# First attention of a four-layer kernel: row units dealt out anew over the twelve steps of a batch

## What is computed

```python
q = hidden @ Wq + bq                       # 56 x 256 a batch, 32 heads of 8
k = encoder @ Wk + bk                      # 1500 x 64, 8 heads of 8
v = encoder @ Wv + bv
scores = einsum('bkgld,bksd->bkgls', q, k) * scale + mask
attn = softmax(scores, axis=-1)            # over the 1500 context rows
out = einsum('bkgls,bksd->bkgld', attn, v)
x = layernorm(out @ Wo + bo + hidden)
```

## Time and profile before

| | |
|---|---|
| median of 3 runs | 3276.99 us (3270.93 to 3280.79) |
| profiled execution | 3270.37 us |
| its span | 3268.5 us |
| mean granted TensorE clock | 0.941 |
| TensorE busy | 2863.0 us (88%) |
| VectorE busy | 2012.5 us (62%) |
| ScalarE busy | 1415.9 us (43%) |
| GpSimd busy | 661.8 us (20%) |

### The profile page before, as it was taken

The page is one execution under the profiler, slowest core; times in us unless marked ns, Lnnn a source line. Parts: engine busy times, 40 slices in busy tenths (PEclk is TensorE's granted clock), DMA queues, the critical chain, the costliest instruction groups (busy, mean ns, idle before and its releaser), DMA issues. The chain is left out here.

```text
span 3268.5 us, 63507 instructions
## 1 busy us (share of the span) xinstructions
PE 2863.0 (88%) x18753; PEld 1515.8 (46%) x18753; DVE 2012.5 (62%) x4195; ACT 1415.9 (43%) x3023; POOL 661.8 (20%) x483
## 2 busy tenths in 40 slices
PE   5799999999999999999867888699999997888885
PEld 3344444444444444444334444356666664544443
DVE  3667677676767767677447887344454440168775
ACT  2255555555555555565622221254544443212221
POOL 5221221121122122112023333000000001033331
PEclk8699999999999999999978999799999998999997
DMA  6333333432433343243010000111111100100000
GB/s 198 106 83 114 108 112 85 121 108 76 120 108 105 91 121 108 75 121 102 16 63 1 1 1 1 47 34 28 33 32 29 32 17 30 60 1 6 6 1 12
DMA packets 117235, 205.18 MB, mean 63 GB/s; under 512 B 39765, under 2 KB 84546, under 8 KB 116546
## 3 DMA queue, kind: packets, MB, share of 16 engines
q1 hardware_dynamic: 116930, 201.08, 21.5%
HBM read 156.09 MB, written 44.59 MB: 61 GB/s over the span
## 5 line engine op out<-in xcount | busy, mean ns | idle before, releaser
L586 DVE CUSTOM_DVE_ANT_0 masked<-ps_a,mask 112x750 f32<-112x750 f32 x1024 | 941.7, 936 | 377.8 <-PE ps_a L473 369.1
L546 ACT ACTIVATE probs<-ps_a 128x448 f32<-128x448 f32 (+1 forms) x1536 | 743.3, 542 | 546.6 <-PE ps_a L439 542.8
L473 PE MATMUL ps_a<-ks,q_row 96*112 96x375 bf16 x2048 | 530.1, 342 | 58.0 <-DVE part_max L586 35.6
L439 PE MATMUL ps_a<-q_sc,ks 99*128 99x448 bf16 (+1 forms) x1536 | 450.5, 359 | 50.0 <-ACT probs L546 28.5
L459 PE MATMUL ps_a<-probs,vp 128*32 128x224 f32 x6144 | 378.4, 364 | 1.2 <-ACT probs L546 0.9
L473 PEld LDWEIGHTS ps_a<-ks,q_row 96*112 96x112 bf16 x2048 | 220.6, 133 | 329.8 <-issue 271.0
L2024 DVE CUSTOM_DVE_ANT_0 f_masked<-ps_c,f_mp 112x432 f32<-112x432 f32 x256 | 145.6, 605 | 221.3 <-PE ps_c L1876 218.7
L439 PEld LDWEIGHTS ps_a<-q_sc,ks 99*128 99x128 bf16 (+1 forms) x1536 | 132.5, 100 | 281.3 <-issue 232.5
L236 POOL CAST k_piece<-kv_t 64x1500 bf16<-64x1500 f32 x32 | 45.6, 1426 | 1042.8 <-ACT kv_t L228 1042.6
L459 PEld LDWEIGHTS ps_a<-probs,vp 128*32 128x32 f32 x6144 | 164.3, 111 | 160.0 <-ACT probs L546 60.8
L215 PE MATMUL ps_a<-ctx_t,wkv 128*128 128x375 f32 x512 | 198.6, 514 | 21.0 <-DVE x_nat L347 10.8
(11 more groups left out here) (283 smaller groups left out, 3978.3 us busy)
## 6 DMA issues: line engine op xcount, KB each, us to landing
ctx_t<-in_ctx_t SPq DMA_DIRECT2D x32, 1500.0 KB, 8.8
ks<-k_scr SPq DMA_DIRECT2D x64, 562.5 KB, 5.1
mask<-in_mask SPq DMA_DIRECT2D x64, 328.1 KB, 5.4
k_scr<-k_piece SPq DMA_DIRECT2D x64, 281.2 KB, 6.5
k_scr<-k_piece SPq DMA_DIRECT2D x64, 187.5 KB, 6.8
f_context<-in_ctx_t SPq DMA_DIRECT2D x32, 375.0 KB, 3.1
k_scr<-k_piece SPq DMA_DIRECT2D x64, 93.8 KB, 7.1
q_row<-q_scr SPq DMA_DIRECT2D x64, 84.0 KB, 4.5
```

The source lines that it names most:

```text
L439: mm = pe.matmul(out, ks[par][:, j, at], q_sc[par][:, j], start=True, stop=not with_mask)
L473: mm = pe.matmul(ps[0:2 * L, bank + i, 0:SC], q_row[which][:, j, h, gp * 2 * L:(gp + 1) * 2 * L], ks[which][0:SROWS, j, at], start=True, s ...
L546: act.activation(probs[t % 2][0:n, i], ps[0:n, k % SCORE_BANKS, 0:PW] .rearrange("p (h n) -> p h n", h=2), ACT.Exp).then_inc(probs_done, 1)
L586: dve.tensor_tensor_reduce(out=masked[:, u % 2], in0=two_banks(bank, 2 * L), in1=in_two(mask[which][:, c * SU:(c + 1) * SU]), scale=1.0, s ...
```

## The change

The table of row units and the order within a step change. Steps 0, 6, 7 and 11 have two row units instead of three, steps 3, 4, 5 and 10 four instead of three; the others keep their number. In the steps with four, one stands at place 0, one at place 1 (ahead of the second score pair), and then at place 2 a row, the `kv` or `out` unit, and the fourth row. In the steps with two, one stands at place 0 and one at place 2, behind the second score pair. Step 9 keeps its three at places 0, 1 and 2. The number of units in the list is 40 before and after, and so is the rule of the two bank pairs.

| step | 0 | 1 | 2 | 3 | 4 | 5 | 6 | 7 | 8 | 9 | 10 | 11 |
|---|---|---|---|---|---|---|---|---|---|---|---|---|
| rows before | 3 | 2 | 2 | 3 | 3 | 3 | 3 | 3 | 1 | 3 | 3 | 3 |
| rows after | 2 | 2 | 2 | 4 | 4 | 4 | 2 | 2 | 1 | 3 | 4 | 2 |
| other unit | | den | turn | kv | out | kv | | | kv | neg | kv | |

```diff
--- before.py
+++ after.py
@@ -51,7 +51,7 @@
 
 
 EARLY_ROWS = 9
-ROWS_AT = {9: 3, 10: 3, 11: 3, 0: 3, 1: 2, 2: 2, 3: 3, 4: 3, 5: 3, 6: 3, 7: 3, 8: 1}
+ROWS_AT = {9: 3, 10: 4, 11: 2, 0: 2, 1: 2, 2: 2, 3: 4, 4: 4, 5: 4, 6: 2, 7: 2, 8: 1}
 OTHERS_AT = {1: ("den", -1, 0), 2: ("turn", 1, 0), 3: ("kv", 3, 0), 4: ("out", -1, 0), 5: ("kv", 3, 1),
              8: ("kv", 3, 2), 10: ("kv", 3, 3)}
 NEG_STEP = 9
@@ -67,10 +67,13 @@
         if t == NEG_STEP:
             units.append((t, 0, "neg", 1, 0))
         units.append((t, 0) + mine[0])
+        rest = mine[1:]
+        if len(rest) == 3 or (len(rest) == 2 and t not in OTHERS_AT):
+            units.append((t, 1) + rest.pop(0))
+        units += [(t, 2) + m for m in rest[:1]]
         if t in OTHERS_AT:
-            units += [(t, 2) + m for m in mine[1:2]] + [(t, 2) + OTHERS_AT[t]] + [(t, 2) + m for m in mine[2:]]
-        else:
-            units += [(t, 1) + m for m in mine[1:2]] + [(t, 2) + m for m in mine[2:]]
+            units.append((t, 2) + OTHERS_AT[t])
+        units += [(t, 2) + m for m in rest[1:]]
     return units
```

## The result

The changed kernel takes 3314.49 us (median of 4 runs, 3312.42 to 3316.19) against 3274.34 (3270.93 to 3280.79): a ratio of 1.0127, 95% interval 1.0107 to 1.0146. It is slower by 40 us, where 22 was forecast (3299, from the median of 3276.99 then known). The time lies inside the stated range (3281 to 3319), but nearer to rival B's 3320 than to the forecast. The profiled span is 3314.3 us, 45.8 longer than before.

What follows compares the result with a forecast made beforehand. TensorE's fixed issue order was taken as bound, held by row banks (1.79 us) and the exponential loop (2.33). Costs 2.98 less savings 2.16 gave 0.82 a batch, +22 with smaller terms: 3299, range 3281 to 3319.

Steps and rivals of the forecast that it cites:

- rival B: ScalarE paces two-row steps; steps 6 to 8 save just 0.74, steps 0 and 1 nothing: +43 us, 3320; 14%.
- the named signs: Key products 1.8 us behind added rows; steps 6, 7: 2.4–2.6; 3, 5, 10: 5.1–5.4; 4: 5.8; batch: 47.6 us.
- Added rows beside key products: Steps 3, 5, 10: product waits for its bank behind the fourth row; 0.67 us each, 2.01 a batch.
- Step 4: Output product starts 1.79 us behind the added row, nothing returns behind it: cost 0.97 us a batch.
- Steps 6 to 8: Two-row steps 6 and 7 lose the row bank's hold; 9.80 us together falls by 1.42.
- What is late next is the exponential loop, 2.33 us, so it just fits: Step 7: scores, exponentials, value product, next scores take 2.33 us, within the forecast step of 2.41.
- Steps 0 and 1: Second scores of step 0 and the accumulator copy come earlier: 0.37 us saved a batch, bounds 0 and 0.55.
- step 11: Last step of a batch, one row unit fewer: saving 0.37 us of 4.18, bounds 0 and 0.45.
- The loop's jump: Step 0 behind the jump, once in four batches at half clock: removed row saves 0.3 more, 1.8 us in all.
- Rival A: Key and output products don't wait on the added row; each four-row step pays just 0.37: -20 us, 3257; 10%.
- Rival C: Additional cold-clock stretches per batch or per four batches, 2.3 us each: +14 to +55, some 3330 with the forecast; 6%.
- Rival D: Little difference: full returns behind key products, larger savings in steps 0 and 1 and 6 to 8: 3280 to 3291; 14%.

Runs made afterwards that it cites:

- Alone: Kernel before with one row unit moved from step 7 to step 4, other steps unchanged: 3283.29 us, ratio 1.0031.
- The half exponential: Changed kernel with ScalarE's exponentials on 224 of 448 columns, the value product taking that half twice: 3291.24 us, ratio 1.0055.
- the last experiment: Kernel before with product first in three-row steps 3, 5, 10, and one mask branch per batch instead of one per score pair: 3476.05 us, ratio 1.0631.
- the first experiment: Changed kernel with the key or output product first behind the second scores in steps 3, 4, 5, 10, both remaining rows after it: 3325.24 us.
- the same order with the branch ahead of each pair: Kernel before, own row counts; in steps 3, 5, 10 second row before second scores, key product right behind them, then third row: 3249.84 us.

## Why the prediction was right in kind and short in size

The four stands came where they were forecast, and the kernel got slower by them. The size was short: batch 22 grew by 1.80 us where the steps summed to 0.82, and that 3314 us is inside the range is owed to an upper bound that had been widened for rival B. Of the named signs, steps 3 and 5 came in their bounds and step 7 at the edge (2.61); steps 6 (2.68), 10 (5.52) and 4 (5.93) and the batch (48.62) came above them. By the prediction's own terms:

- *Added rows beside key products (2.01 forecast):* +0.74, +0.79 and +0.79, 2.32. The hold came as computed, at 1.81 instead of 1.79 (in step 3 at 1.95: the product starts 0.29 behind the end of the read and not 0.16, and why is open). The giving back behind it was smaller: from a held product to the row behind it are 1.34, not 1.26 (1258.38 to 1259.72), and the row of the next step came 2.25 after the product, not 2.19.
- *Step 4 (0.97):* +1.09, the same mechanism. Alone it cost 0.97.
- *Steps 6 to 8 (-1.42):* -0.91. This is the mis-sized term and half of the whole miss of 0.98. The step that failed is "What is late next is the exponential loop, 2.33 us, so it just fits". Another hold sits ahead of that loop, the ring of three score banks: the second matmul of a first pair waits for an exponential that ends 0.94 after its scores went out, and in a two-row step only the other matmul of its pair, one row unit and one score matmul stand between. The prediction had the sign before it, the 0.72 of the pair at 1223.84 in the earlier trace rows, and took the whole 0.74 up to the row for the hold of the row's bank. With that bank free the row comes 0.57 behind the pair in step 7 and 0.62 in step 8, not 0.38, which is 0.43 of the 0.51. In the steps without rows of batch 31 TensorE waits 0.35 for the same exponential and the step still takes 2.33, so there the wait is hidden in the loop; a row at place 0 queues behind it and lengthens the step. The half exponential gave 0.19 of it back in step 8 and 0.16, on the mean, in step 7.
- *Steps 0 and 1 (-0.37):* -0.54, better than forecast; *step 11 (-0.37):* -0.32; steps 2 and 9, put at nothing, cost 0.16 together.
- *The loop's jump (-1.8 in all):* nothing. Step 0 of batch 21 fell by 0.68 (5.02 to 4.34), but step 1 behind it grew by 0.29, where it fell by 0.19 in batch 22; of batches 2 to 24, the five behind a jump grew by 1.58 on the mean, the others by 1.59.

Batch 22 was among the dearer: the first 29 batches grew by 46 us, 1.6 us each, and the span by 45.8.

Rival A (no hold) is out by the waits of 0.57 us. Rival C is out: the granted clock stayed at 1.00 over the whole of batch 22 with its four new stands, and from 150 to 1600 us it is 0.98 on the mean before and after. The Trainium skill, "TensorE: Matmul & The Clock Gate", section "A second HAM failure mode: psum-queue depth-cycling", tells of a kernel in which frequent short idles between groups of matmuls made the clock swing between its two levels. The trace of this case does not show that for four stands of about 0.6 us a batch. Behind the stands of over 4 us in the last experiment the clock did fall. Rival D needed savings of 1.80 in steps 6 to 8 and is out by the 0.91. Rival B has the nearest time and half of its mechanism: it named ScalarE as what shortens the savings in steps 7 and 8, and that happened, through a bank and not through ScalarE's load, which in step 7 is 1.80 us of 2.61 (in step 8, with the read of a key product, 3.09 of 3.60). Its other half, no saving in steps 0 and 1, did not happen: they gave 0.54.

## What to carry to other kernels

Where an engine issues in a fixed order and buffers rotate, a unit's price is set by which unit stands one rotation before it, not by how much slack its step has: write down, for each added unit, who must have read its buffer and whose buffer it now makes late. A step that looks long because of a held unit has no room for another unit; changing the order so that a product stands between two rows of one bank was worth 22 us, dealing out rows by step length cost 40. When one hold goes, look for every other rotation (here the score banks), not just for the longest loop; a pair of matmuls shown for 0.72 us where others take 0.54 is such a rotation at work.

## What the runs showed of the hardware

What a branch of TensorE costs goes by its place. Without the branch ahead of each score pair the order of the first experiment ran 49 us faster: at the turn of a batch the scores came 0.77 us behind the last row instead of 1.54, and 0.34 instead of 0.52 behind a row that had been held. One branch over a whole batch was far worse, with a step 11 of 7.7 us in batch 22, where the same order with the branch ahead of each pair has 4.3, and the clock lowered behind it.
